# The front of a scan-and-experts kernel: one-pass dt products, split input projections, and softplus of batch 0 started inside the convolution

## The reference, cut to what matters

```python
x = einsum('ed,bld->bel', in_proj_w, ctx)            # DI = 512 channels from DM = 256
xc = depthwise_conv(x, conv_w, taps=4)               # causal, along l
u = silu(xc + conv_b)
x_dbl = einsum('ke,bel->bkl', x_proj_w, u)           # 48 rows: dt_lo 16, B 16, C 16
delta = softplus(einsum('er,brl->bel', dt_proj_w, dt_lo) + dt_b)
for t in range(L):                                   # the scan, 16 states for each channel
    state = state * exp(delta_t * A) + (delta_t * u_t) * B_t
    y_t = sum_n(state * C_t)
y = (y + D * u) * silu(layernorm(x))
```

## Time and profile before

| | |
|---|---|
| median of 3 runs | 903.67 us (900.91 to 904.7) |
| the profiled execution | 904.82 us, its span 903.0 us |
| TensorE busy | 809.5 us (90%) |
| VectorE busy | 659.1 us (73%) |
| ScalarE busy | 556.4 us (62%) |
| GpSimd busy | 521.0 us (58%) |
| mean granted TensorE clock | 0.954 |
| softplus chain's last step (delta_u of batch 3 and a copy_du) ends | 111.83 us |

### The profile page before, as it was taken

One profiled execution on the slowest core, in us unless ns is written; L12 is line 12 of the kernel. 1 busy time (PEld: TensorE's weight loads), 2 busy tenths in 40 slices (PEclk: granted clock), 3 DMA queues, 4 the chain that ended last, 5 costly groups with the idle time before them and its releaser, 6 DMA issues.

```text
span 903.0 us, 16039 instructions
## 1 busy us (share of the span) xinstructions
PE 809.5 (90%) x4380; PEld 589.3 (65%) x4381; DVE 659.1 (73%) x858; ACT 556.4 (62%) x927; POOL 521.0 (58%) x326
## 2 busy tenths in 40 slices
PE   6987479999999998999599999999999999999991
PEld 2322378888888887888477768886555555555550
DVE  4857979999999999999767675825655565655550
ACT  3577679999999999998134422123555455554541
POOL 2310059999999999999745542032344535446442
PEclk9966699999999999999699999999999999999996
DMA  5010031112114112110310112159377777788773
GB/s 172 0 52 2 0 118 59 54 53 58 52 51 154 53 58 94 60 36 2 140 73 21 47 48 94 30 180 417 65 186 212 188 224 177 205 190 199 196 161 48
DMA packets 32424, 95.44 MB, mean 106 GB/s; under 512 B 5088, under 2 KB 5216, under 8 KB 29040
## 3 DMA queue, kind: packets, MB, share of 16 engines
q1 hardware_dynamic: 20400, 65.37, 21.0%
q0 software_dynamic: 11968, 29.37, 15.3%
HBM read 122.11 MB, written 21.36 MB: 159 GB/s over the span
## 4 chain that ended last, share of the span: by engine, by line
PE 43%; DMA 17%; DVE 15%; issue 9%; POOL 9%; ACT 5%; POOLq 1%; DVEq 0%; SPq 0%; ACTq 0%
DVE r L983 11%; DMA out<-sg,ids 8%; DMA out<-sb_sb,ids 8%; PE ps L1505 6%; PE ps L1506 6%; PE ps L1507 6%; POOL r L464 5%; PE ps L1430 5%; PE ps L1454 5%; PE ps L1361 3%; PE ps L1431 3%; PE ps L1369 2%; PE ps L1679 2%; PE ps L1660 2%; ACT mem L696 2%
## 5 line engine op out<-in xcount | busy, mean ns | idle before, releaser
L464 POOL TENSOR_TENSOR r<-r,mem 128x1024 f32<-128x1024 f32 x126 | 295.2, 2380 | 57.2 <-DMA mem<-cm_rows 53.9
L983 DVE TENSOR_TENSOR_SCAN r<-r,ps 128x1024 f32<-128x1024 f32 x128 | 286.8, 2276 | 14.8 <-issue 10.6
L684 ACT ACTIVATE r<-mem,nega 128x511 f32<-128x511 f32 x256 | 166.9, 711 | 1.1 <-DVE r L983 1.1
L1430 PE MATMUL ps<-ident,mem 128*128 128x128 f32 x768 | 130.4, 279 | 31.2 <-DVE r L983 21.2
L1454 PE MATMUL ps<-ident,r 128*128 128x128 f32 x1024 | 132.6, 273 | 1.2 <-POOL r L464 1.0
L696 ACT ACTIVATE mem<-mem,bc 128x512 f32<-128x512 f32 x192 | 124.6, 712 | 9.7 <-PE ps L1431 9.2
L1430 PEld LDWEIGHTS ps<-ident,mem 128*128 128x128 f32 x768 | 87.3, 142 | 56.6 <-issue 54.2
L1454 PEld LDWEIGHTS ps<-ident,r 128*128 128x128 f32 x1024 | 115.8, 141 | 2.1 <-POOL r L464 1.5
L1431 PE MATMUL ps<-mem 128*128 128x128 f32 x512 | 100.0, 277 | 0.0
L1679 PE MATMUL ps<-mem 128*128 x188 | 90.5, 605 | 1.5 <-ACT mem L846 0.9
L1660 PE MATMUL ps<-r,picked 128*128 x188 | 88.3, 592 | 0.0
(11 more groups left out here) (195 smaller groups left out, 1316.3 us busy)
## 6 DMA issues: line engine op xcount, KB each, us to landing
r<-in_r_up SPq DMA_DIRECT2D x47, 1024.0 KB
mem<-in_r_down SPq DMA_DIRECT2D x47, 512.0 KB
mem<-cm_rows SPq DMA_DIRECT2D x64, 256.0 KB, 3.2
mem<-in_r_b SPq DMA_DIRECT2D x4, 2048.0 KB, 13.9
r<-in_x SPq DMA_DIRECT2D x4, 1024.0 KB, 5.0
xn_scratch<-r SPq DMA_DIRECT2D x16, 256.0 KB, 3.0
out<-acc POOLq DMA_DIRECT2D x16, 256.0 KB, 3.0
mem<-in_ctx_t SPq DMA_DIRECT2D x4, 512.0 KB, 7.8
```

The costliest lines, as they stand in the source:

```text
L464: pool.tensor_tensor(state[:, k % 2, ec:ec + 2], state[:, k % 2, ec:ec + 2], c, ALU.mult).then_inc(s["weighed"], 1)
L684: act.activation(decay[:, k % 2, ec, 1:L], delta[:, b, ec, 1:L], ACT.Exp, scale=nega[:, ec, n:n + 1]).then_inc(s["decay_ready"], 1)
L983: dve.tensor_tensor_scan(state[:, half, ec:ec + 2].rearrange("p e l -> p (e l)"), decay[:, half, ec:ec + 2].rearrange("p e l -> p (e l)"), ...
L1430: pe.transpose(ps[:, ec, lt * P:(lt + 1) * P], dbu_t[:, k % 2, lt, ec * P:(ec + 1) * P], ident[:])
```

## The change

- `project_dt` multiplies in one fp32r pass over 80 stacked rows. x_dbl has 80 rows: dt, C, dt, B, dt. GpSimd rounds them to fp32r (`x_stack`) and subtracts the rounded from the value in the second copy of dt (`stack_x_dbl`); the weights (`dt_stack`) hold dt_proj three times, the third as its remainder, and zeros at C and B. So one pass sums head x head, rest x head and head x rest.
- x_proj is loaded as five slices of 16 columns into `xproj_sb` (80 columns), dt_proj three times.
- `project_in` for batches 1 to 3 is a split product; GpSimd makes heads and rests of in_proj and ctx (`split_inputs`).
- Batch 0's magnitudes go between the taps of batches 2 and 3; its x_dbl is copied a step earlier; ScalarE waits for all of `loaded_scan` ahead of the first tap.
- The order behind the convolution is written anew on ScalarE, VectorE and TensorE: `first_stats(0)` ahead of `one_and_lost(0)`, `logarithm` and `copy_du` sooner.
- `bc` shrinks to `b_turned`, B's columns alone. The zero rows that GpSimd stores move into `acc`, and GpSimd's last batch of D * u waits for those stores.
- Some semaphores of the router are merged (topf_made, member_made, ids_listed), which leaves the same waits.

```diff
 XD = DR + 2 * DS
+XR = 3 * DR + 2 * DS
+C_AT, DT_REST, B_AT, DT_AGAIN = DR, 2 * DR, 3 * DR, 4 * DR
...
-            sp.dma_start(xproj_sb[:], x_proj_t).then_inc(s["loaded_scan"], 16)
-            sp.dma_start(dtproj_sb[:], dt_proj_t).then_inc(s["loaded_scan"], 16)
+            for at in (0, DT_REST, DT_AGAIN):
+                sp.dma_start(xproj_sb[:, :, at:at + DR], x_proj_t[:, :, 0:DR]).then_inc(s["loaded_scan"], 16)
+            sp.dma_start(xproj_sb[:, :, B_AT:B_AT + DS], x_proj_t[:, :, DR:DR + DS]).then_inc(s["loaded_scan"], 16)
+            sp.dma_start(xproj_sb[:, :, C_AT:C_AT + DS], x_proj_t[:, :, DR + DS:XD]).then_inc(s["loaded_scan"], 16)
+            sp.wait_ge(s["consts_zeroed"], 6)
+            for at in (0, DT_REST, DT_AGAIN):
+                sp.dma_start(dt_raw[at:at + DR], dt_proj_t).then_inc(s["loaded_dt"], 16)
             sp.dma_start(dtb_sb[:], dt_b).then_inc(s["loaded_scan"], 16)
             sp.dma_start(dskip_sb[:], d_skip).then_inc(s["loaded_scan"], 16)
             sp.dma_start(nega[:], a_log).then_inc(s["loaded_scan"], 16)
...
+            pool.memset(dt_raw, 0.0).then_inc(s["consts_zeroed"], 1)
+            pool.wait_ge(s["consts_zeroed"], 6)
...
+            def split_inputs(head, rest_, value, count):
+                pool.tensor_copy(one_pass(head), value).then_inc(s["ctx_split"], 1)
+                pool.wait_ge(s["ctx_split"], count)
+                pool.tensor_tensor(one_pass(rest_), value, head, ALU.subtract).then_inc(s["ctx_split"], 1)
+            def stack_x_dbl(b):
+                pool.wait_ge(s["xd_copied"], b + 1)
+                since(pool, s["dt_ready"], EC * (b - 1))
+                pool.tensor_copy(one_pass(x_stack[0:XR, b % 2]), x_dbl[0:XR, b]).then_inc(s["x_stacked"], 1)
+                pool.wait_ge(s["x_stacked"], 2 * b + 3)
+                rows = slice(DT_REST, DT_REST + DR)
+                pool.tensor_tensor(one_pass(x_stack[rows, b % 2]), x_dbl[rows, b], x_stack[rows, b % 2],
+                                   ALU.subtract).then_inc(s["x_stacked"], 1)
+                pool.wait_ge(s["x_stacked"], 2 * b + 4)
...
+            pool.wait_ge(s["loaded_first"], 16 * 3)
+            split_inputs(inp_head, inp_rest, inp_sb, 1)
+            for b in range(1, B):
+                pool.wait_ge(s[f"ctx_{b}"], 16)
+                split_inputs(ctx_head[b - 1], ctx_rest[b - 1], ctx_sb[:, :, b * L:(b + 1) * L], 2 * b + 1)
+            pool.wait_ge(s["loaded_dt"], 16 * 3)
+            pool.tensor_copy(one_pass(dt_stack[:]), dt_raw).then_inc(s["x_stacked"], 1)
+            pool.wait_ge(s["x_stacked"], 1)
+            rows = slice(DT_AGAIN, DT_AGAIN + DR)
+            pool.tensor_tensor(one_pass(dt_stack[rows]), dt_raw[rows], dt_stack[rows], ALU.subtract).then_inc(s["x_stacked"], 1)
+            pool.wait_ge(s["x_stacked"], 2)
+            pool.wait_ge(s["loaded_scan"], 16 * 8)
             for b in range(B):
+                stack_x_dbl(b)
...
+                if b == B - 1:
+                    pool.wait_ge(s["pad_stored"], 16 * 2)
...
+            act.wait_ge(s["loaded_scan"], 16 * 8)
             last_tap(0)
             for i in range(NT):
                 if i + 1 < NT:
                     last_tap(i + 1)
+                if i == 6:
+                    copy_x_dbl(0)
+                if i == 7:
+                    copy_b(0)
+                if i in (8, 10, 12, 14):
+                    magnitudes(0, (i // 2 - 4,))
+                if i == 11:
+                    copy_x_dbl(1)
+                if i == 13:
+                    copy_b(1)
                 silu(i)
-                if i in (7, 11):
-                    copies(0, 1 if i == 7 else 2)
-                if i == 12:
-                    copies(1, 1)
-                if i == NT - 2:
-                    act.wait_ge(s["loaded_scan"], 16 * 5)
-                    act.wait_ge(s["pad_stored"], 16 * 2)
-                    magnitudes(0, range(2))
-            magnitudes(0, range(2, EC))
...
             exponential(0)
-            copies(1, 2)
-            copies(2, 1)
-            magnitudes(1, range(EC))
-            copies(2, 2)
+            copy_x_dbl(2)
+            magnitudes(1, range(2))
+            logarithm(0)
+            copy_x_dbl(3)
+            magnitudes(1, range(2, EC))
             exponential(1)
-            copies(3, 1)
-            copies(3, 2)
-            logarithm(0)
+            copy_b(2)
+            copy_b(3)
             act.wait_ge(s["relu_less"], 1)
             magnitudes(2, range(EC))
+            copy_du(0)
+            logarithm(1)
             exponential(2)
-            logarithm(1)
             act.wait_ge(s["relu_less"], 2)
             magnitudes(3, range(EC))
+            copy_du(1)
             exponential(3)
-            copy_du(0)
             logarithm(2)
-            copy_du(1)
             logarithm(3)
             copy_du(2)
...
+            first_stats(0)
             one_and_lost(0)
             less_lost(0)
-            first_stats(0)
             first_shift(0)
-            one_and_lost(1)
             add_logarithm(0)
             delta_u(0)
+            one_and_lost(1)
             less_lost(1)
-            one_and_lost(2)
+            copy_du(0)
             add_logarithm(1)
             delta_u(1)
+            one_and_lost(2)
             less_lost(2)
-            copy_du(0)
-            one_and_lost(3)
+            copy_du(1)
             add_logarithm(2)
             delta_u(2)
+            one_and_lost(3)
             less_lost(3)
-            copy_du(1)
+            copy_du(2)
             add_logarithm(3)
             delta_u(3)
-            copy_du(2)
...
+            def project_in(b, ecs=range(EC)):
+                if b > 0:
+                    pe.wait_ge(s["ctx_split"], 2 * (b + 1))
+                    for ec in ecs:
+                        i, cols = b * EC + ec, slice(ec * P, (ec + 1) * P)
+                        since(pe, s["conv_done"], i - 3)
+                        split_product(ps[:, PROJ_BANK[i % 4]],
+                                      [(inp_head[:, mc, cols], inp_rest[:, mc, cols], ctx_head[b - 1][:, mc], ctx_rest[b - 1][:, mc])
+                                       for mc in range(MC)]).then_inc(s["proj_ready"], 1)
+                    return
                 pe.wait_ge(s[f"ctx_{b}"], 16)
-                for ec in range(EC):
+                for ec in ecs:
...
+            def project_dt(b, ecs=range(EC)):
+                pe.wait_ge(s["x_stacked"], 2 * (b + 2))
+                for ec in ecs:
                     since(pe, s["relu_made"], EC * b + ec - 1)
-                    pe.matmul(ps[:, DT_BANK[ec % 2]], dtproj_sb[:, ec * P:(ec + 1) * P], x_dbl[0:DR, b],
+                    pe.matmul(ps[:, DT_BANK[ec % 2]], one_pass(dt_stack[:, ec * P:(ec + 1) * P]), one_pass(x_stack[0:XR, b % 2]),
                               start=True, stop=True).then_inc(s["dt_ready"], 1)
...
+            early, late = range(EC // 2), range(EC // 2, EC)
             project_in(0)
             project_in(1)
-            pe.wait_ge(s["loaded_scan"], 16 * 5)
+            pe.wait_ge(s["loaded_scan"], 16 * 8)
             pe.wait_ge(s["consts_made"], 2)
             project_x(0)
-            project_in(2)
+            project_in(2, early)
             turn_bc(0)
+            project_dt(0, early)
+            project_in(2, late)
             project_x(1)
-            project_in(3)
-            project_dt(0)
+            project_in(3, range(1))
+            project_dt(0, range(2, 3))
+            project_in(3, range(1, 2))
             turn_bc(1)
+            project_dt(0, range(3, 4))
+            project_in(3, late)
             project_x(2)
-            project_dt(1)
+            project_dt(1, early)
+            project_x(3)
             turn_bc(2)
-            project_x(3)
+            project_dt(1, late)
             turn_bc(3)
             project_dt(2)
-            project_dt(3)
             pe.wait_ge(s["conv_done"], NT)
             turn_du(0)
+            project_dt(3)
             turn_du(1)
             turn_du(2)
```

More of the change, by code:

```diff
@@ L96, in bass_xattn_scan_moe_kernel @@
         d_u = acc[:].rearrange("p t d -> p (t d)").rearrange("p (b e l) -> p b e l", e=EC, l=L)
-        no_rows = view(rd, 7680, D)
+        no_rows = acc[:, NT - 1]
+        dt_raw = acc[0:XR, NT - 2]
+        x_stack = view(split_t, 5 * T // 2, 2, L)
+        ctx_head, ctx_rest = (tuple(view(split_d, 2 * i * MC * L + part * MC * L, MC, L) for i in range(B - 1)) for part in range(2))
+        inp_head, inp_rest = (view(split_d, (2 * (B - 1) + part) * MC * L, MC, DI) for part in range(2))
         conv = view(r0, 8192, 4, L)
@@ L261, in bass_xattn_scan_moe_kernel @@
         names = """
-        waits_passed loaded_first loaded_scan loaded_b1 loaded_b2 loaded_shared loaded_sup loaded_sdown
+        waits_passed loaded_first loaded_dt loaded_scan ctx_split x_stacked loaded_b1 loaded_b2 loaded_shared loaded_sup loaded_sdown
         ctx_0 ctx_1 ctx_2 ctx_3
@@ L334, in _ @@
```

(37 more changed lines are left out.)

34 lines of the change are left out of this document (14 added, 20 removed).

## The result

| | before | after |
|---|---|---|
| median (runs) | 903.67 us (5) | 908.35 us (5) |
| lowest to highest | 900.91 to 906.67 | 908.28 to 910.95 |
| profiled execution, its span | 904.82, 903.0 | 908.33, 906.4 |
| first tap | 11.85 | 18.58 |
| the convolution's last product ends | 50.09 | 55.09 |

The ratio is 1.0062, 95% interval 1.0032 to 1.0091: slower, by 0.6%. The time lies 4.2 us over the forecast and inside the range; of the three cases it is the one that had a chance of 0.20.

A forecast was written before the change was run, and what follows sets the result against it. The prediction took the front before the scan (convolution, hole, VectorE's softplus chain, ending at 111.8) to decide the shift: -6.2 there plus 6.75 for the later start gives +0.55 on 903.67, so 904.2 us; range 899.5 to 910.5.

The forecast's parts named there:

- the one that had a chance of 0.20: Whole kernel: the case slower, by more than 0.5% (4.5 us); same had 0.71, faster 0.09.
- start: Ahead of the convolution: the first tap waits for nega, the last small load, until 18.6; all behind it 6.75 us later.
- convolution: 16 tiles, 12.66 to 50.09 before: split projections cut the 1.66 us hole at tile 12 to some 0.65; gain 1.0.
- hole: Convolution's end to one_and_lost(0): x's load and the statistics now set it, 57.9 instead of 58.50 without the later start.
- softplus chain: VectorE's four batches ahead of the scan: 47.7 us instead of 53.3, bounds 45.1 and 50.2.
- the two bounds of the start: First tap: 15.1 at the earliest, as nega landed before, and 23.3 at the latest.
- The rival of transfers paid in turn: Small weight loads: six added transfers each pay a fixed cost in turn; start at 27, sum +9, or 31 and +13.
- 0.65 us of lateness at tile 12: Convolution: tile 12 still waits some 0.65 us for TensorE's projections and project_x(1).
- TensorE at half clock: Convolution, at project_x(0): TensorE at 1.2 GHz after a pause, 3.5 us more, 0.7 of it slack; 907.0; chance 0.14.
- 45.1 us if solid: Softplus chain: VectorE's own steps for four batches without any wait, 45.1 us.
- waits of 1.5, 0.3 and 0.8: Softplus chain: 1.5 us for logarithm(1), 0.3 for logarithm(2), 0.8 for dt products and turns at half clock.
- One-pass dt products do nothing by themselves: Softplus chain: probably no gain of their own, as VectorE waits for ScalarE, and ScalarE only in part for them.

The follow-up runs named there:

- e1: Changed kernel, but ScalarE waits for loaded_scan just ahead of copy_x_dbl(0), not ahead of the first tap; 900.03 us, 0.9976 of the kernel before.
- f3: Changed kernel with the edits of e1 and e2, but batches 1 to 3 projected in fp32 again; 899.2 us, 0.9953 of the kernel before.
- g2: Changed kernel with the edits of e1 and e2, but batch 0's magnitudes behind silu 15 as before; 903.1 us, 0.9988 of the kernel before.
- h1: g2 with all products by D made ahead of batch 2's stack on GpSimd; 896.81 us, 0.9933 of the kernel before.
- f2: Changed kernel with the edits of e1 and e2, and one_and_lost(0) ahead of first_stats(0); 897.22 us, 0.9912 of the kernel before.
- e2: Changed kernel, but GpSimd makes rstd_first(0) ahead of the last stack, stack_x_dbl(3); 903.29 us, 1.0001 of the kernel before.
- g1: f4 with GpSimd's stacking of x_dbl dropped too, the dt products waiting for copy_x_dbl alone; 902.78 us, 1.0002 of the kernel before.
- f4: Changed kernel with the edits of e1 and e2, but dt products in fp32 again, stacking kept; 904.34 us, 1.002 of the kernel before.

## Why the prediction was right or wrong, point by point

The terms of the sum, measured from the traces and in brackets as forecast: start +6.7 (+6.75), convolution -1.7 (-1.0), hole +0.4 (+0.4), softplus chain -1.7 (-5.6); in all +3.75 (+0.55). The range held because it was set by the two bounds of the start; the overrun came from another term.

- **The start: right, +6.7 for +6.75, by two errors that cancel.** The tap came at 18.58, forecast 18.6, released by nega. But SP, not the transfer engines, set it: a 512-piece transfer holds SP for 1.2 to 1.9 us and not some 1.2, and nega then landed after 2.0, less than the 2.7 that I took for the least. The rival of transfers paid in turn (a start at 27 or later) did not happen; e1 shows that the place of the wait was the whole price.
- **The convolution: gain 1.7 for 1.0.** I left 0.65 us of lateness at tile 12; there was none. The terms as I wrote them even add up to only 0.4 (7.1 against 6.69). f3 gives the split projections 2.0 us. GpSimd's splits are hidden: copies of 1.04 us, below the 1.3 that I set as their least, and subtractions of 2.34.
- **The hole: right.** 5.58 us of waiting for x, `one_and_lost(0)` 8.85 us after the last product for 8.8. g2 and h1 show the step that carried this, that x and no longer ScalarE bounds the hole; f2, which doesn't wait for x there, has `one_and_lost(0)` 4.35 us after the last product for the sum's 4.4.
- **TensorE at half clock: it came where the rival put it, and had no price.** The clock was at 0.50 from 23 to 26 us, but back before `project_x(0)` (starts 0.43 us apart). Over the whole chain the granted clock was 0.63, before 0.66. The 0.8 us that I added for it in the chain can't be seen in VectorE's rows.
- **The softplus chain: this is the step that failed.** The text has "45.1 us if solid" and waits of 1.5, 0.3 and 0.8: 47.7, at most 50.2. It took 51.6. Of the three waits 0.15 is left, and there is one that isn't in the sum, 5.94 for rstd. The 45.1 was right. I worked out when ScalarE's and TensorE's results come, and took GpSimd as hidden because its splits are; I did not follow the one small step that GpSimd makes for this chain through the queue into which `stack_x_dbl` was put. It was to be found in the change itself: `stack_x_dbl(3)` waits for `copy_x_dbl(3)`, and that one stands behind `logarithm(0)`. e2 takes the wait away: its front ends at 111.79 where my sum has 112.35 (57.9 + 47.7 + 6.75), and its median is 903.29 where my sum has 904.2. That nearness is partly luck: e2's chain takes 48.2 for my 47.7, but with 0.3 us of waits and 2.5 of stretched rows, which I did not have, in place of my 2.6 of waits.
- **"One-pass dt products do nothing by themselves": wrong.** In the new order they carry 7.1 to 7.9 us, 7.8 to 9.3 with the scatter of the start (g1, f4). I had judged them by the old order; there too ScalarE waited for each fp32 product, but no copy of VectorE's stood behind it so early. It did not hurt the sum, since the change has them.
- **Which rival came.** Slower, but not by the way that I had priced: the start was on time, and the loss came from a queue of an engine called hidden.
